# Second attention of a two-layer model: per-token head scores in 32x32 strips instead of 128x128 blocks, and one copy out of PSUM instead of four

## The reference

```python
Q = (x @ Wq.T).reshape(b, s, h, hd)      # h = 16 heads of hd = 16
K = (x @ Wk.T).reshape(b, s, h, hd)
V = (x @ Wv.T).reshape(b, s, h, hd)
scores = einsum('bshd,bstd->bsht', Q, K) / sqrt(hd)   # a 16x16 matrix for each token
attn = softmax(scores, axis=-1)
out = einsum('bsht,bstd->bshd', attn, V).reshape(b, s, dm)
return out @ Wfc.T
```

## Time and profile before

| | before |
|---|---|
| median of 3 runs | 1005.07 us (1004.25 to 1008.22) |
| the profiled execution | 1004.16 us, span 1002.2 us |
| busy in the span | PE 938.0 us (94%), PEld 789.9 (79%), DVE 705.5 (70%), ACT 492.3 (49%), POOL 322.4 (32%) |
| scores, L1814 | 1024 records of mean 290 ns, 549 to 754 us |
| picks, L1649 | 128 of mean 587 ns, 550 to 756 us |
| transposes, L1570 | 128 of mean 702 ns |
| mean granted PE clock | 0.981 |

### The profile page before, as it was taken

How to read it: one execution, slowest core, us unless ns; L and a number is a source line. 1 busy time by engine, 2 the same in 40 slices (tenths; PEclk the granted TensorE clock), 3 DMA queues, 4 the chain that set the end, 5 groups by cost and what they waited for, 6 DMA issues and landing times. The chain is left out here.

```text
span 1002.2 us, 29936 instructions
## 1 busy us (share of the span) xinstructions
PE 938.0 (94%) x11260; PEld 789.9 (79%) x11261; DVE 705.5 (70%) x1820; ACT 492.3 (49%) x1325; POOL 322.4 (32%) x288
## 2 busy tenths in 40 slices
PE   6899999989999999999999999999888879999996
PEld 3466666888999999999987788887777778888775
DVE  3567886883777777777650679898989779466552
ACT  2556666322545454545435878787754450222221
POOL 0034533513232323232220334343443100555552
PEclk9999999999999999999999999999979899999998
DMA  9784582277322222222116757766651630443440
GB/s 337 204 363 126 132 261 83 85 275 233 95 88 88 86 94 85 93 80 94 54 28 119 142 104 135 164 137 140 118 122 56 256 150 1 144 141 119 132 139 34
DMA packets 130473, 133.76 MB, mean 133 GB/s; under 512 B 73692, under 2 KB 118878, under 8 KB 128180
## 3 DMA queue, kind: packets, MB, share of 16 engines
q1 hardware_dynamic: 119764, 90.82, 32.5%
q0 software_dynamic: 10592, 41.30, 12.9%
HBM read 94.27 MB, written 44.11 MB: 138 GB/s over the span
## 5 line engine op out<-in xcount | busy, mean ns | idle before, releaser
L1212 PE MATMUL psall<-rows 128*128 128x128 f32 x1248 | 146.0, 275 | 1.9 <-ACT rows L1359 1.1
L1212 PEld LDWEIGHTS psall<-rows 128*128 128x128 f32 x1248 | 144.0, 192 | 3.3 <-ACT rows L1359 1.3
L1226 PE MATMUL psall<-whi,rows 128*128 x624 | 141.0, 379 | 0.0
L1226 PEld LDWEIGHTS psall<-whi,rows 128*128 128x128 f32 x624 | 115.7, 190 | 14.1
L1178 POOL DMA_INDIRECT attn_rows<-rows,tok_i x39 | 41.7, 1069 | 184.4 <-DVE rows L1335 184.4
L287 PE MATMUL psall<-cst 128*128 128x128 f32 x752 | 96.1, 286 | 0.6 <-PEq L1451 0.6
L1570 DVE STREAM_TRANSPOSE whi<-whi 32x512 f32<-32x512 f32 x128 | 89.9, 702 | 5.9 <-POOL whi L1529 3.8
L287 PEld LDWEIGHTS psall<-cst 128*128 128x128 f32 x752 | 91.8, 200 | 1.7 <-issue 1.3
L1365 ACT ACTIVATE rows<-psall,vs 128x128 f32<-128x128 f32 x312 | 84.9, 383 | 6.0 <-PE psall L1212 3.6
L1649 ACT ACTIVATE whi<-psall 32x512 f32<-32x512 f32 x128 | 75.2, 587 | 14.8 <-PE psall L1814 12.5
L1301 DVE COPY rows<-wlo 128x2048 f32 (+1 forms) x39 | 47.5, 1219 | 47.5 <-PE psall L1212 42.5
(11 more groups left out here) (299 smaller groups left out, 1808.9 us busy)
## 6 DMA issues: line engine op xcount, KB each, us to landing
ffn_rows<-mod_rows SPq DMA_DIRECT2D x2, 4096.0 KB
wlo<-attn_rows SPq DMA_DIRECT2D x64, 128.0 KB, 3.0
wlo<-in_W SPq DMA_DIRECT2D x2, 4096.0 KB, 17.7
whi<-in_w SPq DMA_DIRECT2D x5, 1024.0 KB
whi<-mod_rows SPq DMA_DIRECT2D x4, 1024.0 KB, 13.7
ffn_rows<-rows SPq DMA_DIRECT2D x8, 512.0 KB
ffn_rows<-x SPq DMA_DIRECT2D x8, 512.0 KB
v_turn<-wlo SPq DMA_DIRECT2D x32, 128.0 KB, 3.6
```

What stands on the lines that cost most here:

```text
L1212: last = eng.matmul(b_up[t.par][f // 4][:, (f % 4) * P:(f % 4 + 1) * P], w_now[:, c, f * P:(f + 1) * P], inT[t.par][:, c * P:(c + 1) * P], ...
L1226: last = eng.matmul(b_dn[t.par][:, 0:D], hidT[t.par][:, f * P:(f + 1) * P], w_down[:, bass.ds(e, 1), f, :].rearrange("p o n -> p (o n)"), ...
```

## The change

The scores of a group of eight tokens are computed two tokens by two: 32 columns of queries against the 32 columns of keys of the same two tokens. Pair q of the group writes partitions 32q to 32q + 31, k writes bank k, columns 256 + 32g to 256 + 32g + 31. A tile has 64 such matmuls of 32x32 instead of 16 of 128x128, and what lies in PSUM afterwards is, in each bank, 128 partitions by 128 columns without anything unwanted. The pick is one copy of 128 x (4 x 128) = 128x512. The two half calls of it become one, at the place of the first.

```diff
@@ -1408,7 +1408,7 @@
 
         def one_of(two_and_last, t):
             return two_and_last[t % 2 if t < FIRST_LAST else 2 + t - FIRST_LAST]
-        b_s = psall[:, 0:4 * 512].rearrange("p (g n) -> p g n", g=GR)
+        b_s = psall[:, 0:4 * 512].rearrange("p (k n) -> p k n", k=TB)[:, :, D:D + P]
         b_y = [ps[k][:, 0:D] for k in range(TB)]
         b_qk = [ps[4], ps[5]]
         b_T = ps[6][:, 0:D]
@@ -1420,7 +1420,7 @@
         v_d = nc.dram_tensor("v_turn", [NT, P, D], F32).ap()
 
         LAG_N, LAG_SHIFT, LAG_V, LAG_KEEP_V, LAG_QK, LAG_KEEP_QK, LAG_Y, LAG_TURN_H = 1, 2, 3, 3, 5, 6, 15, 20
-        LAG_PV, LAG_LG, LAG_TURN_LG, LAG_S, LAG_COMP, LAG_COMP_REST, LAG_EX, LAG_OT = 14, 20, 21, 10, 11, 11, 12, 15
+        LAG_PV, LAG_LG, LAG_TURN_LG, LAG_S, LAG_COMP, LAG_EX, LAG_OT = 14, 20, 21, 10, 11, 12, 15
         LAG_H1T, LAG_KEEP_LG, LAG_KEEP_TURNED, LAG_RSTD, LAG_H, LAG_SUM, LAG_MX, LAG_GATE = 20, 21, 21, 19, 18, 11, 11, 14
         LAG_STAT, LAG_ET, LAG_NORM, LAG_SUB, LAG_X, LAG_NLD, LAG_VST, LAG_VLD = 17, 12, 13, 12, 18, 0, 5, 9
         LAG_KT, LAG_XLD, LAG_ROW, LAG_ST = 7, 15, 16, 20
@@ -1640,16 +1640,10 @@
                     wait_some(eng, c_["ss"], TB * (b - 1))
                     eng.activation(zqk[b % 2][:, :, 4 * i:4 * i + 4], b_qk[t % 2].rearrange("p (h t) -> p t h", h=4), ACT.Copy).then_inc(c_["qke"], 1)
 
-                def compact(quads, done):
-                    def stage(t):
-                        eng.wait_ge(c_["ss"], t + 1)
-                        wait_some(eng, c_["et"], t - 2)
-                        for q in quads:
-                            rows_q = slice(32 * q, 32 * q + 32)
-                            last = eng.activation(sc[t % 3][rows_q], b_s[rows_q, :, 32 * q:32 * q + 32], ACT.Copy)
-                        if done:
-                            last.then_inc(c_["comp"], 1)
-                    return stage
+                def compact(t):
+                    eng.wait_ge(c_["ss"], t + 1)
+                    wait_some(eng, c_["et"], t - 2)
+                    eng.activation(sc[t % 3].rearrange("p (k g) n -> p k (g n)", k=TB), b_s, ACT.Copy).then_inc(c_["comp"], 1)
 
                 def exps(t):
                     eng.wait_ge(c_["sub"], t + 1)
@@ -1681,17 +1675,16 @@
                 def keep_logits(t):
                     eng.wait_ge(c_["ll"], t - FIRST_LAST + 1)
                     eng.activation(key3[:, t, :], b_lg[t - FIRST_LAST], ACT.Copy)
-                compact_first, compact_rest = compact((0, 1), False), compact((2, 3), True)
                 tile_steps([(LAG_KEEP_LG, keep_turned_logits), (LAG_KEEP_QK, keep_qk), (LAG_OT, keep_oT),
-                            (LAG_SHIFT, shift_h), (LAG_RSTD, rstd2), (LAG_COMP, compact_first), (LAG_H1T, keep_h1T),
-                            (LAG_KEEP_V, keep_v), (LAG_COMP_REST, compact_rest),
+                            (LAG_SHIFT, shift_h), (LAG_RSTD, rstd2), (LAG_COMP, compact), (LAG_H1T, keep_h1T),
+                            (LAG_KEEP_V, keep_v),
                             (LAG_KEEP_TURNED, keep_group_logits), (LAG_EX, exps)],
-                           [(LAG_KEEP_LG, keep_turned_logits), (LAG_OT, keep_oT), (LAG_COMP, compact_first),
-                            (LAG_COMP_REST, compact_rest), (LAG_KEEP_V, keep_v),
+                           [(LAG_KEEP_LG, keep_turned_logits), (LAG_OT, keep_oT), (LAG_COMP, compact),
+                            (LAG_KEEP_V, keep_v),
                             (LAG_KEEP_TURNED, keep_group_logits), (LAG_RSTD, rstd2), (LAG_SHIFT, shift_h),
                             (LAG_EX, exps), (LAG_KEEP_QK, keep_qk), (LAG_H1T, keep_h1T)])
-                compact_first(30); keep_oT(26); rstd2(22); compact_rest(30); keep_oT(27); exps(29); compact_first(31)
-                compact_rest(31); keep_h1T(21); rstd2(23); exps(30); keep_h1T(22); keep_oT(28); keep_oT(29); keep_h1T(23)
+                compact(30); keep_oT(26); rstd2(22); keep_oT(27); exps(29); compact(31)
+                keep_h1T(21); rstd2(23); exps(30); keep_h1T(22); keep_oT(28); keep_oT(29); keep_h1T(23)
                 keep_turned_logits(23); rstd2(24); exps(31); keep_h1T(24); keep_group_logits(23); rstd2(25); keep_oT(30)
                 keep_oT(31); rstd2(26); rstd2(27); keep_h1T(25); keep_h1T(26); keep_h1T(27); rstd2(28); rstd2(29)
                 rstd2(30); keep_turned_logits(27); keep_h1T(28); rstd2(31); keep_group_logits(27); keep_h1T(29); keep_h1T(30)
@@ -1809,10 +1802,11 @@
                     wait_some(eng, c_["ya"], TB * put["project"])
                     put["scores"] += 1
                     for g in range(4):
-                        for k in range(TB):
-                            at, tok = slice(k * QD, k * QD + HD), slice(32 * p + 8 * g, 32 * p + 8 * g + 8)
-                            last = eng.matmul(b_s[:, 4 * k + g, :], zqk[b % 2][at, tok, :].rearrange("p t h -> p (t h)"),
-                                              zk[b % 2][at, tok, :].rearrange("p t h -> p (t h)"), start=True, stop=True)
+                        for q in range(4):
+                            for k in range(TB):
+                                at, two = slice(k * QD, k * QD + HD), slice(32 * p + 8 * g + 2 * q, 32 * p + 8 * g + 2 * q + 2)
+                                last = eng.matmul(b_s[32 * q:32 * q + 32, k, 32 * g:32 * g + 32], zqk[b % 2][at, two, :].rearrange("p t h -> p (t h)"),
+                                                  zk[b % 2][at, two, :].rearrange("p t h -> p (t h)"), start=True, stop=True)
                     last.then_inc(c_["ss"], 1)
                 b_unread = ps[5][:, 3 * P:4 * P]
                 b_unread_late = ps[3][:, 3 * P:4 * P]
```

## The result

The changed kernel takes 1089.64 us, the median of 4 runs (1087.93 to 1091.0), against 1004.66 us of the kernel before in the same comparison (4 runs, 1002.16 to 1008.22). The ratio is 1.0835, 95% interval 1.0802 to 1.0868: slower by 85 us. The span of the profiled execution went from 1002.2 to 1086.0 us, 83.8 us more. The PE group of L287 with which the second expert layer begins stood at 789.52 us and now stands at 873.11, 83.6 us later: all of it lies in the second attention.

A forecast was written before the change was run, and what follows sets the result against it. PE and DVE set the pace, with PE's instruction fetch as third limit. 67 blocks at 4.1 us add 56 us, long projection work 13, less 5: +64 on 1004.2 gives 1068 us, range 1014 to 1108.

The forecast's parts named there:

- a third limit: Second attention: PE's program comes in blocks of 256 instructions, each taking about 4.1 us to arrive.
- (a): ACT's four picks become one, 1.76 us less per tile; worth 0 on the path, bounds 0 and -8 us.
- (b): Scores on PE: 128 records at 9.0 ns take 1.34 us instead of 1.17, 0.17 us more per tile.
- (c): PE's code in the second attention: 192 more instructions per tile, 6144 in all, 24 more blocks, 43 becoming 67.
- The sum, +64 us: Second attention: +56 us for fetching blocks, +13 for long projection work, -5 for waits and cuts already there.
- The term of 4.1 us per block: Shortest time per fetched PE block, ends 3.4 and 4.8; 67 blocks take 275 us instead of 219, +56.
- long work in them: Blocks holding a projection need 1.6 us beyond 4.1 us, for each of 8 projections, 13 us.
- took off 5: PE's 3.0 us of waiting for ACT and part of today's cuts vanish behind a slower PE, -5 us.
- the clock: PE's granted clock may drop after cuts, but the slower array mostly fills waiting time: 0, bounds 0 and +25 us.
- Fetching keeps up: Rival: blocks are requested further ahead, so only 0.17 us per tile counts, 5 us, 1009 us; chance 0.12.
- faster: Rival: the array takes small strips 0.47 us faster per tile and fetching keeps up, 996 us; chance 0.08.
- Row strips slow: Rival: score records take 29 to 36.6 ns, PE's work grows 80 to 112 us, about 1095 us; chance 0.10.

The follow-up runs named there:

- the quarter form: The changed kernel with only 16 of the 64 strip matmuls per tile (pair q = 0 alone): 999.16 us, ratio 0.9932.
- the loops: The changed kernel with 64 strip matmuls per tile run from looped code: 31 twice plus 2, 1044.03 us; 15 four times plus 4, 1034.52 us.

## Why the prediction was right, point by point

**What bounds the kernel.** Right: a third limit beside PE and DVE, in no busy time, and the change ran into it.

**(a) ACT's pick, 0 us, bounds 0 and -8.** Right: -4 alone in the old kernel, -5 in the new one, there within the noise.

**(b) The scores' array time, 1.34 us.** Right in the uncut group (1.37, and 1.30 to the next group). The rule of the Trainium skill (TensorEngine Tiling (Array Packing), Instruction Overhead), by which it would be 3.2 us, does not hold for these records: the first 52 in the group at 643.19 are (0.65 - 0.21) / 51 = 8.6 ns apart (0.21 is the mean of one), far under 60 cycles, which are 25 ns at 2.4 GHz.

**(c) 24 more blocks.** Exact, 82 to 106 packets. What the Trainium skill (Runtime: NRT & Kernel Launch, Instruction fetch mechanics) calls mostly hidden is hidden in the kernel before, whose blocks last 5.1 us, but for 5.8 us put to "issue" between 549 and 757. It is less so in the quarter form (18.5 us, 46 packets from 538 to 757), and not in the changed kernel (40.5 us in the same window, 57 in its whole stage).

**The sum, +64 us, was 20 us short**; measured 84 in the span, 81 of them in the 67 blocks (300 us instead of 219). The term of 4.1 us per block was right where the fetch decides: the 40 blocks that end in a cut last 2.2 to 6.1 us, 4.14 on average. The 27 that end without one last 4.98. The sum had 275 us for the blocks, 13 for long work in them, and took off 5: 283 us, 17 short of the 300. Taking off the 5 was wrong in itself, since the waits of the kernel before lie in the 219 that are subtracted and not in the 275.

Most of the rest goes with the clock, which I set to 0 with +25 as its end. The 38 blocks that ran at 2.4 GHz throughout last 4.02 us on average, the 29 with a piece at 1.2 GHz in them 5.08, 31 us more over the 29. In the stage the granted clock was 0.86 on average instead of 0.96, and groups of unchanged work grew by 15.8 (queries and keys), 4.2 (weighing) and 6.0 us (values), 26 us together. No run holds the clock, so how much of the 20 us it costs by itself is not shown.

My argument was that a slower array only fills the time in which PE waits for code. That fails in blocks with much array work: 17 of the 29 blocks with the lower clock end without a cut, 5.37 us on average, and the one with the values at 2.08 us and L1734 at 3.64 is 6.8 us long. The forecast's own range, 1022 to 1108, holds the result. Its upper end is that of a slow fetch, 4.8 us per block (+103 us), which did not come; with the clock's own bound of +25 the sum reaches 89, and the measured 84 lie inside that as well.

**Rivals.** Fetching keeps up (1009) and faster (996) fell by the cuts inside the scores: with 24 more packets the fetching did not keep up. With the old instruction count and a quarter of the matmuls the new form does run at 999. Row strips slow (1095) gave nearly the measured time with the wrong cause: a time alone would not have told them apart, the whole group of 1.37 us and the loops do.

**What would show it.** Records x4096, 106 packets and PE's fall from 98% to 78% in the middle were as said; DVE fell from 93% to 61%, further than the 70% forecast. Two signs were off in size. Idle time put to "issue" was 1.8 us per tile (57 over 32 tiles), not about 1. The packets were not 4 us apart all along, but 3.4 to 9.1 us.

## What to carry to other kernels

Count PE's instructions per microsecond, not only its busy time: an fp32 matmul is four of them, and here a run of 256 in less than about 4 us made PE wait for its own program, in idle time that the profile puts to "issue". Divide the length of a stage by the instruction queue's packets in it, look for groups cut in two, and check that the cuts are a multiple of 256 instructions apart; then splitting matmuls to save another engine's work costs a fetch for each 64 fp32 matmuls. Behind idle time of PE the granted clock was lower (0.86 on average instead of 0.96 in this stage), and work that had not changed was busy 26 us longer.

## What the runs showed of the hardware that was not expected

Code that repeats is not fetched again: 64 matmuls per tile from 19 in the code, 15 of them in a loop, took 84 packets instead of 106, and a pass of the loop cost PE about 0.2 us. Alternating between row strips (16 x 128) and column strips (128 x 32) in groups of 8 and 16 records cost 1.2 us per tile against two groups on end, 0.14 us for each change of form. With the small strips (16 x 32, 32 records, then 16 of the column strips) a round took 0.27 + 0.59 us, 3.44 per tile against 1.30 + 1.78 = 3.08, which is 0.4 us per tile: the price is not the same for all forms.
